# Scoring the last four heads of each attention batch as three fp32r products of split operands

## The chip, the cores and the metric

One core of one Trainium2 chip runs the whole program. The metric is the device time of one launch in microseconds; times given as a median come from several launches. Its engines are TensorE (PE, with its weight loads as PEld), VectorE (DVE), ScalarE (ACT), GpSimd (POOL) and SyncE (SP), which issues most of the DMAs.

## The reference

A batch of 64 sequences of 32 rows and 512 columns goes through three small linear maps whose weights are picked by an index of each sequence, and then through an attention layer with a paged cache. Attention is the part that matters here:

```python
q = rope(rmsnorm(x @ Wq)); k = rope(rmsnorm(x @ Wk)); v = x @ Wv
kc = k_cache[block_table].reshape(bsz, 512, 8, 128)
vc = v_cache[block_table].reshape(bsz, 512, 8, 128)
k_all = concatenate([kc, k], axis=1)
v_all = concatenate([vc, v], axis=1)
scores = einsum('bqhd,bkhd->bhqk', q, k_all) * SCALE
scores = where(valid, scores, -1e30)
probs = softmax(scores, axis=-1)
o = einsum('bhqk,bkhd->bqhd', probs, v_all)
return o.reshape(bsz, 32, 32 * 128) @ Wo.T
```

There are 32 query heads over 8 key heads, so four query heads of 32 rows share a key head and form 128 rows. Each sees 512 cached keys and 32 new ones, 544 in all. Everything is float32.

## The kernel before

The program runs its stages one after the other: preparation, maps, values, projection, attention, output. The change lies in `stage_attention`.

That stage walks over the 64 sequences, which are called batches here, two to a loop iteration (a pair). A pair has 16 steps `n`, one per key head; `j` is the batch within the pair and `h` the head, 0 to 7. Buffers that are kept twice are numbered by `j`. Each engine has its own written-out order of work and waits on semaphores for the others; nothing is reordered.

- **SP** loads, per batch, 16 key pages of 128 KB each and the new keys (L1056, L1057), the queries (L1058), then the new values of the batch before (L1065), and stores a finished batch (L1071). Key and query buffers are reused two batches on, so the load waits until the last head of the batch that used them is scored.
- **POOL** loads the cached values of the next batch with four indirect DMAs in heads 3 to 6 (L1106, L1110). In every head it multiplies the exponentials by the reciprocal of their sum (L1124), and every fourth head it does so for the 32 new keys of four heads together (L1129).
- **TensorE** in step n makes the scores of head n (L1147), turns the weights of head n-2 (L1157, every fourth head also the group of new ones, L1164), and weighs the values of head n-3 (L1179, every fourth head also the new values, L1188). The scores are two float32 products of 288 and 256 key columns, each of which becomes two matmul instructions on the chip.
- **DVE** takes the scores out of PSUM with the mask and the row minimum (L1273), copies the turned weights of head n-2 out of PSUM (L1283), and makes the reciprocal of head n's sum (L1287). In head 7 it also makes the mask of the next batch (L1256 to L1259).
- **ACT** makes the exponentials and their sum (L1214), copies the turned new weights (L1225) and the finished outputs (L1235) every fourth head.

The scores and the turned weights have two PSUM buffers each, and the exponentials a ring of eight. The output stage and the projection already multiply in this way: float32 operands are kept as a rounded high part and a low part, both of type fp32r, and three fp32r products are summed in PSUM (L1430, L824). ACT makes a high part by a copy (L1466), DVE a low part by a subtraction (L1487, L887).

## Time and profile before

| | us |
|---|---|
| median of 3 runs | 2527.35 (2525.82 to 2528.05) |
| the profiled execution, whole | 2534.27 |
| its span, first to last instruction | 2532.5 |
| TensorE busy in the span | 2423.1 |
| DVE, ACT, POOL busy | 1545.5, 1161.6, 1124.4 |
| attention stage, scores of the first to the last batch | about 851 to 2141 |
| mean granted TensorE clock, share of full | 0.983 |

The rows of a trace name the engine, the line of the kernel, the operation, and output and inputs by the program's names. Busy time of an engine is the sum of its instructions without overlap; matmuls are pipelined, so the distance between two starts says more of their price than the duration of one. Where an engine waits for a semaphore, the trace names the instruction that released it.

### The profile page before, as it was taken

What the parts mean: (1) busy time and instruction counts of PE and PEld (TensorE: products, weight loads), DVE (VectorE), ACT (ScalarE), POOL (GpSimd) and SP (SyncE); (2) the same over time, 40 slices, a digit from 0 to 9 for tenths busy, and PEclk for the clock granted to TensorE, in tenths of its full rate; (3) what the DMA queues carried; (4) which work ended last, traced back from release to release, by engine and by line L of the source; (5) the groups of instructions that cost most, each with busy time, mean ns of one, the idle gap of its engine ahead of it and who ended that gap; (6) DMA issues with size and microseconds to landing.
All of it is one profiled execution on the core that took longest, in us unless ns stands there. A gap on an engine that the chain in (4) does not pass through costs nothing. (4 is left out here: it accounts for less than half of the span.)

```text
span 2532.5 us, 52304 instructions
## 1 busy us (share of the span) xinstructions
PE 2423.1 (96%) x14785; PEld 2023.1 (80%) x14785; DVE 1545.5 (61%) x3027; ACT 1161.6 (46%) x2251; POOL 1124.4 (44%) x1364
## 2 busy tenths in 40 slices
PE   5989999999999599999999999999999999899999
PEld 4337777777776498999998999999989998788887
DVE  4656299888888466666666666666666665332221
ACT  6663387778777233433433344344333433321111
POOL 0323144444444466666666666666656665000000
PEclk9999999999999799999999999999999999999999
DMA  9334233333332788888888888888888885843442
GB/s 307 100 102 170 82 104 104 93 100 98 95 94 86 229 275 270 273 274 275 271 272 269 276 274 275 274 273 276 278 254 274 275 272 179 241 126 107 133 126 65
DMA packets 475258, 501.44 MB, mean 198 GB/s; under 512 B 104373, under 2 KB 399285, under 8 KB 471094
## 3 DMA queue, kind: packets, MB, share of 16 engines
q1 hardware_dynamic: 438326, 366.38, 47.2%
q0 software_dynamic: 36864, 134.23, 16.1%
q8 instruction: 32, 0.52, 0.1%
q14 instruction: 36, 0.29, 0.0%
HBM read 404.02 MB, written 96.47 MB: 198 GB/s over the span
## 5 line engine op out<-in xcount | busy, mean ns | idle before, releaser
L1214 ACT ACTIVATE att_probs<-att_probs,att_low 128x544 f32<-128x544 f32 x512 | 383.2, 748 | 800.9 <-DVE att_low L1273 798.6
L1124 POOL TENSOR_TENSOR att_probs<-att_probs,att_inverse 128x512 f32<-128x512 f32 x512 | 534.4, 1044 | 392.1 <-DVE att_inverse L1287 388.7
L1273 DVE CUSTOM_DVE_ANT_0 att_probs<-att_score,att_mask,att_batch_cols 128x544 f32<-128x544 f32 x512 | 401.5, 784 | 340.7 <-PE att_score L1147 336.7
L1147 PE MATMUL att_score<-att_keys_raw,att_queries_raw 128*128 128x288 f32 (+1 forms) x2048 | 556.5, 395 | 29.9 <-DMA att_queries_raw<-q_t 29.9
L1179 PE MATMUL att_o<-att_probs_t,att_values 128*128 128x128 f32 x4096 | 541.0, 275 | 0.0
L1179 PEld LDWEIGHTS att_o<-att_probs_t,att_values 128*128 128x128 f32 x4096 | 497.6, 192 | 0.1
L1147 PEld LDWEIGHTS att_score<-att_keys_raw,att_queries_raw 128*128 128x128 f32 x2048 | 351.8, 192 | 85.4 <-DMA att_queries_raw<-q_t 31.0
L1283 DVE COPY att_probs_t<-att_turn 128x512 f32<-128x512 f32 x512 | 351.2, 686 | 1.3 <-PE att_turn L1157 1.3
L1157 PE MATMUL att_turn<-ident,att_probs 128*128 128x128 f32 x2048 | 307.8, 273 | 1.6 <-POOL att_probs L1124 1.5
L1157 PEld LDWEIGHTS att_turn<-ident,att_probs 128*128 128x128 f32 x2048 | 256.1, 141 | 54.5 <-POOL att_probs L1124 3.4
L1110 POOL DMA_INDIRECT att_values<-L_cond_v_cache,att_v_rows_of x256 | 251.5, 982 | 81.6 <-POOL att_v_rows_of L1106 49.7
L824 PE MATMUL proj_proj<-x3t_hi,proj_w_hi 128*128 128x512 f32 x640 | 266.5, 416 | 0.0
L824 PE MATMUL proj_proj<-x3t_hi,proj_w_lo 128*128 128x512 f32 x640 | 250.8, 392 | 0.0
L824 PE MATMUL proj_proj<-x3t_lo,proj_w_hi 128*128 128x512 f32 x640 | 250.1, 391 | 0.0
L970 POOL TENSOR_TENSOR proj_q_out<-proj_by_cos,proj_by_sin 128x512 f32<-128x512 f32 x128 | 165.3, 1292 | 172.6 <-DVE proj_by_sin L902 172.6
L1430 PE MATMUL out_y<-out_wot_hi,out_o_hi 128*128 128x512 f32 x512 | 200.2, 391 | 0.0
L1430 PE MATMUL out_y<-out_wot_lo,out_o_hi 128*128 128x512 f32 x512 | 199.4, 390 | 0.0
L1430 PE MATMUL out_y<-out_wot_hi,out_o_lo 128*128 128x512 f32 x512 | 199.4, 389 | 0.0
L1487 DVE TENSOR_TENSOR out_o_lo<-out_o_raw,out_o_hi 128x2048 fp32r<-128x2048 f32 x32 | 73.3, 2291 | 181.7 <-ACT out_o_hi L1466 181.7
L1287 DVE RECIPROCAL att_inverse<-att_total 128x1 f32<-128x1 f32 x512 | 83.4, 163 | 138.5 <-ACT att_probs L1214 138.5
L1466 ACT ACTIVATE out_o_hi<-out_o_raw 128x2048 fp32r<-128x2048 f32 x32 | 61.4, 1919 | 214.5 <-PE out_y L1430 181.3
L900 DVE TENSOR_TENSOR proj_by_cos<-proj_raw,rope 128x512 f32<-128x512 f32 x160 | 136.8, 855 | 37.5 <-ACT proj_raw L856 37.5
(130 smaller groups left out, 3204.7 us busy)
## 6 DMA issues: line engine op xcount, KB each, us to landing
att_keys_raw<-L_cond_k_cache SPq DMA_DIRECT2D x1024, 128.0 KB
q_t<-proj_q_out SPq DMA_DIRECT2D x32, 1024.0 KB, 3.9
att_queries_raw<-q_t SPq DMA_DIRECT2D x64, 512.0 KB
o_t<-att_heads_out SPq DMA_DIRECT2D x64, 512.0 KB, 5.3
out_o_raw<-o_t SPq DMA_DIRECT2D x32, 1024.0 KB, 5.8
prep_natural<-L_cond_weight SPq DMA_DIRECT2D x16, 1024.0 KB, 8.6
w_nat<-L_cond_Wq SPq DMA_DIRECT2D x8, 1024.0 KB, 5.9
v_new<-values_v_out SPq DMA_DIRECT2D x16, 512.0 KB, 2.6
```

What stands on the lines that cost most here:

```text
L824: last = nc.tensor.matmul(proj_ps[t % RING][:], w[u][:, m, c, :], x[:, c, rc * 512:(rc + 1) * 512], start=(c == 0 and k == 0), stop=(c == ...
L900: nc.vector.tensor_tensor(by_cos[n][:], raw[n][:], rope[:, cos, cols], ALU.mult)
L970: nc.gpsimd.tensor_tensor(out, by_cos[n].rearrange("d (b s) -> d b s", s=S), by_sin[n].rearrange("d (b s) -> d b s", s=S), ALU.add).then_i ...
L1110: nc.gpsimd.indirect_dma_start(values[v][:, t, :], None, v_rows, bass.IndirectOffsetOnAxis(ap=v_rows_of[v][:, t:t + 1], axis=0)).then_inc( ...
L1124: nc.gpsimd.tensor_tensor(probs[:, k, 0:L], probs[:, k, 0:L], inverse[:, k:k + 1].to_broadcast([P, L]), ALU.mult).then_inc(probs_ready, 1)
L1147: last = nc.tensor.matmul(score_ps[n % 2][:, cols], queries_raw[j][:, h, :], keys_raw[j][:, pages, h, :], start=True, stop=True)
L1157: last = nc.tensor.transpose(turn_ps[job % 2][:, t * P:(t + 1) * P], probs[:, m % RING, t * P:(t + 1) * P], ident[:])
L1179: last = nc.tensor.matmul(o[:, cols], values[j][:, t, h * D:(h + 1) * D], probs_t[m % 2][:, t * P:(t + 1) * P], start=(h % GH == 0 and t = ...
L1214: nc.scalar.activation(probs[:, k, :], probs[:, k, :], ACT.Exp, bias=low[k][:, 0:1], scale=-1.0, accum_out=total[k][:, 0:1]).then_inc(exp_ ...
L1273: nc.vector.tensor_tensor_reduce(out=probs[:, k, :], in0=score_ps[n % 2][:, LEFT:LEFT + KEYS], in1=mask[j][:], scale=batch_cols[j][:, h:h ...
L1283: nc.vector.tensor_copy(probs_t[m % 2][:], turn_ps[job % 2][:]).then_inc(kept[job % 2], 1)
L1430: last = nc.tensor.matmul(y_ps[g][:], o[h % 2][:, r, rows].rearrange("d b s -> d (b s)"), w[:, hq, :], start=(hq == 0 and k == 0), stop=(h ...
```

## The change

Heads 4 to 7 of a batch (from `NATIVE` on) are no longer scored from the float32 keys and queries. Each operand is kept as a high and a low part of type fp32r, and per product of 288 or 256 columns three matmuls are summed: high by high, query high by key low, query low by key high. The parts of a batch are made in six pieces: five of pages (3, 3, 3, 4 and 4 pages of the four heads, so 384 or 512 columns) and one of queries (512 columns). ACT copies the high parts, pieces 0 to 3 in heads 4 to 7 of the batch before and pieces 4 and 5 in heads 0 and 1 of the batch itself. DVE subtracts for the low parts one head later each, pieces 0 to 2 in heads 5 to 7 and 3 to 5 in heads 0 to 2. TensorE waits before head 4 for all low parts. The mask of the next batch moves from head 7 to head 4 on DVE. SP's key load waits for head 4 of the batch that used the buffer, not head 7. For the first batch ACT makes pieces 0 to 3 and DVE 0 to 2 ahead of the loop; the last pair is written out, since it splits no next batch.

```diff
@@ -982,6 +982,11 @@
     GH = 4
     RING = 8
     PAIRS = B // 2
+    NATIVE = 4
+    ACT_FROM, DVE_FROM = 4, 5
+    SPLIT = HK - NATIVE
+    PARTS = [slice(0, 3), slice(3, 6), slice(6, 9), slice(9, 13), slice(13, NPP + 1)]
+    NP = len(PARTS)
     FIRST = NPP // 2 + 1
     LEFT = 512 - FIRST * PSIZE
     KLD = 16 * (NPP + 2)
@@ -993,6 +998,10 @@
         pages_sb = a_.sb("pages", [1, B * NPP], I32)
         keys_raw = [a_.sb(f"keys_raw{v}", [P, NPP + 1, HK, PSIZE]) for v in range(2)]
         queries_raw = [a_.sb(f"queries_raw{v}", [P, HK, P]) for v in range(2)]
+        keys_hi = [a_.sb(f"keys_hi{v}", [P, NPP + 1, SPLIT, PSIZE], F32R) for v in range(2)]
+        keys_lo = [a_.sb(f"keys_lo{v}", [P, NPP + 1, SPLIT, PSIZE], F32R) for v in range(2)]
+        queries_hi = [a_.sb(f"queries_hi{v}", [P, SPLIT, P], F32R) for v in range(2)]
+        queries_lo = [a_.sb(f"queries_lo{v}", [P, SPLIT, P], F32R) for v in range(2)]
         values = [a_.sb(f"values{v}", [P, PPT, KVD]) for v in range(2)]
         new_values = [a_.sb(f"new_values{v}", [P, HK, D]) for v in range(2)]
         v_rows_of = [a_.sb(f"v_rows_of{v}", [P, PPT], I32) for v in range(2)]
@@ -1014,6 +1023,8 @@
         pages_loaded = a_.sem("pages_loaded")
         keys_loaded = a_.sem("keys_loaded", 2)
+        hi_ready = a_.sem("hi_ready")
+        lo_ready = a_.sem("lo_ready")
         v_loaded = a_.sem("v_loaded", 2)
         new_loaded = a_.sem("new_loaded", 2)
         zeroed = a_.sem("zeroed")
@@ -1051,7 +1062,7 @@
                 if not first:
                     sp.wait_ge(pages_loaded, 16)
-                    sp.wait_ge(scores_done[1], (i - 1) * (N // 2) + (v + 1) * (HK // 2))
+                    sp.wait_ge(scores_done[NATIVE % 2], (i - 1) * (N // 2) + v * (HK // 2) + (NATIVE // 2 + 1))
                 for n in range(NPP):
                     sp.dma_start(keys_raw[v][:, n], kt[bass.ds(pages[n], 1)].rearrange("n d h k -> d (n h) k")).then_inc(keys_loaded[v], 16)
                 sp.dma_start(keys_raw[v][:, NPP], kn_dram[bass.ds(b, 1)].rearrange("b d h s -> d (b h) s")).then_inc(keys_loaded[v], 16)
@@ -1142,10 +1153,18 @@
                 j, h = divmod(n, HK)
                 if h == 0:
                     pe.wait_ge(keys_loaded[j], i * KLD + KLD)
+                if h == NATIVE:
+                    pe.wait_ge(lo_ready, i * (2 * NP + 2) + (j + 1) * (NP + 1))
                 pe.wait_ge(scores_masked[n % 2], i * (N // 2) + n // 2)
                 for pages, cols in ((slice(0, FIRST), slice(LEFT, 512)), (slice(FIRST, NPP + 1), slice(512, LEFT + KEYS))):
-                    last = nc.tensor.matmul(score_ps[n % 2][:, cols], queries_raw[j][:, h, :], keys_raw[j][:, pages, h, :],
-                                            start=True, stop=True)
+                    if h < NATIVE:
+                        last = nc.tensor.matmul(score_ps[n % 2][:, cols], queries_raw[j][:, h, :], keys_raw[j][:, pages, h, :],
+                                                start=True, stop=True)
+                        continue
+                    s = h - NATIVE
+                    for k, (q, kt_) in enumerate(((queries_hi, keys_hi), (queries_hi, keys_lo), (queries_lo, keys_hi))):
+                        last = nc.tensor.matmul(score_ps[n % 2][:, cols], q[j][:, s, :], kt_[j][:, pages, s, :],
+                                                start=(k == 0), stop=(k == 2))
                 last.then_inc(scores_done[n % 2], 1)
             def turn(i, n):
@@ -1208,6 +1227,15 @@
         @block.scalar
         def _(act):
+            def split(b, i, c, v):
+                if c == 0:
+                    act.wait_ge(keys_loaded[v], i * KLD + KLD)
+                if c < NP:
+                    nc.scalar.activation(keys_hi[v][:, PARTS[c]], keys_raw[v][:, PARTS[c], NATIVE:HK], ACT.Copy).then_inc(hi_ready, 1)
+                else:
+                    nc.scalar.activation(queries_hi[v][:], queries_raw[v][:, NATIVE:HK], ACT.Copy).then_inc(hi_ready, 1)
             def softmax(i, n):
                 act.wait_ge(scores_masked[n % 2], i * (N // 2) + (n // 2 + 1))
                 k = n % RING
@@ -1235,22 +1263,43 @@
                 nc.scalar.activation(heads_out[j][:, (g % 2) * GH:(g % 2 + 1) * GH].rearrange("d h n -> d (h n)"), o_ps[g % 2][:],
                                      ACT.Copy).then_inc(o_ready[g % 2], 1)
-            def pair(i, first):
+            def pair(i, first, last_pair):
                 for n in range(N):
+                    j, h = divmod(n, HK)
                     softmax(i, n)
+                    if HK - ACT_FROM + h <= NP:
+                        split(i * 2 + j, i, HK - ACT_FROM + h, j)
+                    if h >= ACT_FROM and not (last_pair and j == 1):
+                        if h == ACT_FROM:
+                            act.wait_ge(scores_done[1], i * (N // 2) + j * (HK // 2))
+                        split(i * 2 + (j + 1), i + j, h - ACT_FROM, (j + 1) % 2)
                     if n % GH == 1 and (n >= GH or not first):
                         new_part(i, n - 2)
                     if n % GH == 3 and (n >= GH or not first):
                         keep_o(i, n - 4)
-            pair(0, True)
-            with act.Fori(1, PAIRS) as i:
-                pair(i, False)
+            act.wait_ge(zeroed, 2)
+            for c in range(HK - ACT_FROM):
+                split(0, 0, c, 0)
+            pair(0, True, False)
+            with act.Fori(1, PAIRS - 1) as i:
+                pair(i, False, False)
+            pair(PAIRS - 1, False, True)
             new_part(PAIRS, -1)
             keep_o(PAIRS, -1)
         @block.vector
         def _(dve):
+            def split(b, c, v):
+                dve.wait_ge(hi_ready, b * (NP + 1) + (c + 1))
+                if c < NP:
+                    nc.vector.tensor_tensor(keys_lo[v][:, PARTS[c]], keys_raw[v][:, PARTS[c], NATIVE:HK], f32(keys_hi[v][:, PARTS[c]]),
+                                            ALU.subtract).then_inc(lo_ready, 1)
+                else:
+                    nc.vector.tensor_tensor(queries_lo[v][:], queries_raw[v][:, NATIVE:HK], f32(queries_hi[v][:]),
+                                            ALU.subtract).then_inc(lo_ready, 1)
             def columns(b, v):
                 cols = stat[:, bass.ds(b, 1), :].rearrange("p b c -> p (b c)")
                 nc.vector.reciprocal(batch_cols[v][:, 0:HK], cols[:, 0:HK])
@@ -1292,8 +1341,12 @@
                     mask_scores(i, n, first)
                     if n >= 2 or not first:
                         main_part(i, n - 2)
+                    if HK - DVE_FROM + h <= NP:
+                        split(i * 2 + j, HK - DVE_FROM + h, j)
                     if not (last_pair and j == 1):
-                        if h == HK - 1:
+                        if h >= DVE_FROM:
+                            split(i * 2 + (j + 1), h - DVE_FROM, (j + 1) % 2)
+                        elif h == DVE_FROM - 1:
                             dve.wait_ge(scores_masked[1], i * (N // 2) + j * (HK // 2))
                             columns(i * 2 + (j + 1), (j + 1) % 2)
                     invert(i, n)
@@ -1304,6 +1357,8 @@
                 nc.vector.memset(mask[v][:, L:KEYS], 0.0).then_inc(setup, 1)
             dve.wait_ge(setup, 3)
             columns(0, 0)
+            for c in range(HK - DVE_FROM):
+                split(0, c, 0)
             pair(0, True, False)
             with dve.Fori(1, PAIRS - 1) as i:
                 pair(i, False, False)
```

TensorE, heads 2 to 4 of a batch in the first pair. `att_turn` is the turn, `att_o` the weighing. Before:

```order
L1188 MATMUL att_o<-att_new_probs_t,att_new_values 128x128 x4
L1147 MATMUL att_score<-att_keys_raw,att_queries_raw 128x288
L1147 MATMUL att_score<-att_keys_raw,att_queries_raw 128x256
L1157 MATMUL att_turn<-ident,att_probs 128x128 x4
L1179 MATMUL att_o<-att_probs_t,att_values 128x128 x4
L1147 MATMUL att_score<-att_keys_raw,att_queries_raw 128x288
L1147 MATMUL att_score<-att_keys_raw,att_queries_raw 128x256
L1157 MATMUL att_turn<-ident,att_probs 128x128 x4
```

The same place now:

```order
L1207 MATMUL att_o<-att_new_probs_t,att_new_values 128x128 x4
L1161 MATMUL att_score<-att_keys_raw,att_queries_raw 128x288
L1161 MATMUL att_score<-att_keys_raw,att_queries_raw 128x256
L1176 MATMUL att_turn<-ident,att_probs 128x128 x4
L1198 MATMUL att_o<-att_probs_t,att_values 128x128 x4
L1166 MATMUL att_score<-att_keys_hi,att_queries_hi 128x288
L1166 MATMUL att_score<-att_keys_lo,att_queries_hi 128x288
L1166 MATMUL att_score<-att_keys_hi,att_queries_lo 128x288
L1166 MATMUL att_score<-att_keys_hi,att_queries_hi 128x256
L1166 MATMUL att_score<-att_keys_lo,att_queries_hi 128x256
L1166 MATMUL att_score<-att_keys_hi,att_queries_lo 128x256
L1176 MATMUL att_turn<-ident,att_probs 128x128 x4
```

Head 3 is scored as before; head 4 has six matmuls where two products stood, and turn and weighing keep their places.

DVE, heads 4 and 5 of the second batch of the first pair, as it is now (ISA stands for the masking and its minimum):

```order
L1322 ISA att_probs,att_low<-att_score,att_mask,att_batch_cols 128x544 [waits att_scores_done0,att_setup,att_turned1]
L1322 ISA att_low 128x1
L1332 COPY att_probs_t<-att_turn 128x512 [waits att_weighed0,att_turned0]
L1305 RECIPROCAL att_batch_cols<-stat 128x8 [waits att_scores_masked1]
L1306 COPY att_batch_cols<-stat 128x1
L1308 TENSOR_SCALAR att_mask<-att_key_no,att_batch_cols 128x512 [waits att_cols_ready]
L1336 RECIPROCAL att_inverse<-att_total 128x1 [waits att_exp_done]
L1322 ISA att_probs,att_low<-att_score,att_mask,att_batch_cols 128x544 [waits att_scores_done1,att_setup]
L1322 ISA att_low 128x1
L1332 COPY att_probs_t<-att_turn 128x512 [waits att_weighed1,att_turned1]
L1297 TENSOR_TENSOR att_keys_lo<-att_keys_raw,att_keys_hi 128x384 [waits att_hi_ready]
L1336 RECIPROCAL att_inverse<-att_total 128x1 [waits att_exp_done]
```

The subtraction stands between the copy out of PSUM and the reciprocal, and the three mask instructions stand in head 4 where before they stood in head 7.

ACT, heads 4 to 6 there, now:

```order
L1242 ACTIVATE att_probs,att_total<-att_probs,att_low 128x544 [waits att_scores_masked0]
L1235 ACTIVATE att_keys_hi<-att_keys_raw 128x384 [waits att_keys_loaded0,att_scores_done1]
L1242 ACTIVATE att_probs,att_total<-att_probs,att_low 128x544 [waits att_scores_masked1]
L1235 ACTIVATE att_keys_hi<-att_keys_raw 128x384
L1253 ACTIVATE att_new_probs_t<-att_turn 128x128 [waits att_o_done0,att_turned0]
L1242 ACTIVATE att_probs,att_total<-att_probs,att_low 128x544 [waits att_scores_masked0]
```

The first copy of the next batch's keys waits for their load, right behind the exponentials of head 4, and the exponentials of head 5 come behind it.

## Rows read from the trace of the kernel before

**Rows 1.** The page, busy time: share of the span and instructions of each engine.
```profile
PE 2423.1 (96%) x14785; PEld 2023.1 (80%) x14785; DVE 1545.5 (61%) x3027; ACT 1161.6 (46%) x2251; POOL 1124.4 (44%) x1364
```

**Rows 2.** Windows: stretch, its length, busy us of each engine, granted clock, DMA share, GB/s.
```profile
291.00:301.00 10.00, 7.70 (x27) 6.22 (x28) 3.46 (x5) 2.99 (x5) 0.20 (x1) 0.50 0.16 51
1400.00:1800.00 400.00, 400.00 (x2922) 367.08 (x2921) 259.80 (x700) 160.48 (x400) 262.51 (x300) 1.00 0.88 275
1878.00:1882.00 4.00, 4.00 (x19) 3.43 (x19) 0.86 (x3) 0.03 (x1) 0.00 (x0) 0.57 0.28 113
```

**Rows 3.** Timeline of TensorE near the attention's end: start us, us, engine, line, operation.
```profile
2089.26 1.06 PE L1188 MATMUL att_o<-att_new_probs_t,att_new_values 128*128 128x128 f32 x8
...
2102.40 1.08 PE L1147 MATMUL att_score<-att_keys_raw,att_queries_raw 128*128 128x288 f32 x4
2103.32 0.60 PE L1157 MATMUL att_turn<-ident,att_probs 128*128 128x128 f32 x4
2103.76 1.06 PE L1179 MATMUL att_o<-att_probs_t,att_values 128*128 128x128 f32 x8
2104.65 1.08 PE L1147 MATMUL att_score<-att_keys_raw,att_queries_raw 128*128 128x288 f32 x4
...
2109.26 1.06 PE L1188 MATMUL att_o<-att_new_probs_t,att_new_values 128*128 128x128 f32 x8
```

**Rows 4.** Timeline of TensorE, output stage: first and last of ten fp32r matmuls.
```profile
2299.83 0.39 PE L1430 MATMUL out_y<-out_wot_hi,out_o_lo 128*128 128x512 f32 x1
...
2301.87 0.39 PE L1430 MATMUL out_y<-out_wot_hi,out_o_lo 128*128 128x512 f32 x1
```

**Rows 5.** Timeline of one head in mid stage; in brackets idle time before and its releaser.
```profile
1512.75 1.05 POOL L1124 TENSOR_TENSOR att_probs<-att_probs,att_inverse 128x512 f32<-128x512 f32 x1
1512.90 0.78 DVE L1273 CUSTOM_DVE_ANT_0 att_probs<-att_score,att_mask,att_batch_cols 128x544 f32<-128x544 f32 x1 [0.49 <-PE att_score L1147]
...
1513.61 0.69 DVE L1283 COPY att_probs_t<-att_turn 128x512 f32<-128x512 f32 x1
1513.73 0.75 ACT L1214 ACTIVATE att_probs<-att_probs,att_low 128x544 f32<-128x544 f32 x1 [1.36 <-DVE att_low L1273]
...
1514.60 0.16 DVE L1287 RECIPROCAL att_inverse<-att_total 128x1 f32<-128x1 f32 x1 [0.31 <-ACT att_probs L1214]
...
1514.95 1.05 POOL L1124 TENSOR_TENSOR att_probs<-att_probs,att_inverse 128x512 f32<-128x512 f32 x1
```

**Rows 6.** Waits of TensorE in the whole run: total us, times, longest us.
```profile
PE att_score L1147 <- DMA att_queries_raw<-q_t: 29.9, 2, 29.1
...
PE att_o L1188 <- DMA att_new_values<-v_new: 7.9, 5, 2.7
...
PE proj_w L794 <- PEq L471: 4.4, 1, 4.4
...
PE att_turn L1157 <- POOL att_probs L1124: 1.5, 3, 0.8
```

**Rows 7.** Groups by form, whole run: busy us, mean ns of one.
```profile
L970 POOL TENSOR_TENSOR proj_q_out<-proj_by_cos,proj_by_sin 128x512 f32<-128x512 f32 x128 | 165.3, 1292 | 172.6 <-DVE proj_by_sin L902 172.6
L900 DVE TENSOR_TENSOR proj_by_cos<-proj_raw,rope 128x512 f32<-128x512 f32 x160 | 136.8, 855 | 37.5 <-ACT proj_raw L856 37.5
...
L1430 PEld LDWEIGHTS out_y<-out_wot_hi,out_o_hi 128*128 128x128 f32 x512 | 96.4, 188 | 19.8
...
L1487 DVE TENSOR_TENSOR out_o_lo<-out_o_raw,out_o_hi 128x2048 fp32r<-128x2048 f32 x32 | 73.3, 2291 | 181.7 <-ACT out_o_hi L1466 181.7
...
L887 DVE TENSOR_TENSOR proj_w_lo<-proj_w,proj_w_hi 128x512 fp32r<-128x512 f32 x40 | 27.5, 688 | 46.4 <-ACT proj_w_hi L844 46.3
```

**Rows 8.** Timeline at the end of the first batch.
```profile
861.46 0.75 ACT L1214 ACTIVATE att_probs<-att_probs,att_low 128x544 f32<-128x544 f32 x1 [1.17 <-DVE att_low L1273]
...
868.57 0.60 PE L1157 MATMUL att_turn<-ident,att_probs 128*128 128x128 f32 x4
...
870.89 1.18 PE L1147 MATMUL att_score<-att_keys_raw,att_queries_raw 128*128 128x288 f32 x4 [0.82 <-DMA att_queries_raw<-q_t]
```

## The prediction

> **What bounds the kernel now.** I read four views in this order: the busy shares, the windows, the timeline of TensorE, then the waits. TensorE is busy 96% of the span, the other engines 44 to 61% [rows 1]. In the middle of the attention stage it is busy all the time, at full granted clock, with DVE at 65%, ACT at 40%, POOL at 66% and the DMA engines at 88% [rows 2]. The timeline shows what fills it [rows 3]. The four matmul instructions that the two score products of a head become take 0.92 us (2102.40 to 2103.32), the turn 0.44 and the weighing 0.89, so a head takes 2.25. Four heads with their group turn and new-value products take 10.00, a batch of eight 20.00 (2089.26 to 2109.26). So each microsecond taken from the scores counts until another engine's work per batch, or a chain of waits, gets as long.
>
> The chain of one head [rows 5]: mask at 1512.90, exponent at 1513.73, reciprocal at 1514.60, POOL's product from 1514.95 to 1516.00, 3.1 us from the end of the scores to weights that can be turned. TensorE turns head n-2 after the scores of head n, two heads (4.5 us) later, so 1.4 us are spare. TensorE waited for POOL 1.5 us in the whole run [rows 6].
>
> **1. Scores of heads 4 to 7.** A native head's 0.92 us is four times its 544 columns at 2.4 GHz (2176 columns, 0.907) and a little. A split head makes six fp32r matmuls; by the 512-wide rows below each goes through once: 3 x 288 and 3 x 256 columns, 1632, 0.680 us at 2.4 GHz. What stands on top of each is not shown at this width. The only fp32r rows are 512 wide: nine intervals in 2.04 us (2299.83 to 2301.87), 0.2267 each, where 512 columns are 0.2133: 13.3 ns more [rows 4]. If that is a fixed price per matmul, a split head costs 0.680 + 6 x 0.0133 = 0.76, and saves 0.16. If it is a share (1/16), 0.72, saving 0.20. As the native rows have it (13 ns over four), 0.70, saving 0.22. Against it: keys are now read in runs of 32 columns at one column per tick, which no row shows; I bound that by half the overhead again, 0.80, saving 0.12. I take 0.16, by the nearest row of the same type. Of 256 split heads, the four of the first batch lie under a DMA wait (3). 252 x 0.16 = **-40.3 us** (ends -30 and -55).
>
> The Trainium skill (TensorE: Matmul & The Clock Gate, "Wait — 56ns, not 53.3ns?") gives N / 2.4 + 2.5 ns between warm matmuls. By it a split head would be an estimated 0.695 us, and this term -57. It also gives 215.8 ns for 512 columns, where this trace has 226.7, so I hold to the row.
>
> **2. New values come earlier.** TensorE waited five times, 7.9 us, for the new values [rows 6]. SP issues them behind the next batch's keys. These now go out once the fifth head's scores are done, not the eighth's, 6.7 us earlier, and the longest wait was 2.7. I take **-7.9 us** (ends 0 and -7.9).
>
> **3. The first batches.** ACT now reads the next batch's keys right behind the exponent of the fifth head. In the first batch that exponent starts at 861.46, but the second batch's keys only land at 870.8: TensorE waited for them until 870.89 [rows 8]. The exponent of head 5 is queued behind that wait and one copy (about 0.5): 871.3. Then 0.85 exponent with its accumulator, 0.2 reciprocal, 1.05 POOL, with hand-overs 873.5. TensorE turns head 5 then, not at 868.57 [rows 8]. Weighing (0.89) and turn (0.44) bring the second batch's first score to 874.9 instead of 870.89: **+4.0**. TensorE idles over 5 us there. After a wait of 4.4 us the clock was at its lower level, 1.2 GHz, in 291 to 301; after one of 2.7 us it was so for part of 1878 to 1882 [rows 2, 6]. I add **+3.0** for work at half clock (ends 0 and 5). Before the first head, four copies and three subtractions (about 2 us) lie beside its first scores, which run at half clock. I expect no such wait for the third batch's keys, whose request moves up by three heads.
>
> **4. What is hidden.** DVE: 259.8 us in 20 batches [rows 2] is 13.0 per batch. A subtraction of 512 columns is 0.69 and one of 2048 is 2.29 [rows 7], so 384 columns are 0.69 - 128 x 0.00104 = 0.56. Three of each add 3.7, sum 16.7, and the batch becomes 20.0 - 4 x 0.16 = 19.36. In one head: the copy out of PSUM ends at 1514.30, and the reciprocal waits for ACT until 1514.60 [rows 5]; a subtraction between them fills the 0.3 and delays the reciprocal by 0.3 to 0.4. The chain is then 3.5 us, two split heads are 4.2: cost nothing, 0.7 left. Without that cover each delay counts directly. The mask columns move from head 7 to 4, where no subtraction lies.
> ACT: six copies, each below the 0.75 exponent of 544 columns [rows 5], under 4.5 beside 8.0 busy per batch: nothing.
> POOL: a head with a value load takes 2.20 (1512.75 to 1514.95) [rows 5], more than a split head's 2.09. But TensorE's three heads there also hold a group turn and new-value products, 7.3 against 6.6. Nothing.
> The wait for the low parts, before head 4's first score: the last subtraction is made in head 2, some 2 us before. Nothing is queued behind it but TensorE's own work.
> DMA: the same bytes, 88% x 20.0 / 19.36 = 91%. The keys' window is the same: before, eighth head's scores to first score two batches on, 20.0 + 1.3 = 21.3; now from the fifth head's scores to ACT's fifth head one batch on, 19.4 + 1.8 = 21.2. Before, no key load was waited for past the second batch [rows 6]. But the value loads, issued in heads 3 to 6, now lie beside the keys' whole first half.
>
> **The sum:** -40.3 - 7.9 + 4.0 + 3.0 = -41.2 us. The profiled execution took 2534.27, so 2493.1; it stands 6.9 above the median of three, 2527.35. From the median: **2486 us**.
>
> **Rivals.**
> *A, slower: VectorE becomes the bound.* The subtraction of two SBUF operands may stand off against POOL's product. In the projection stage DVE's product of two SBUF operands takes 855 ns beside POOL's 1292, where a 512-column subtraction with a PSUM operand takes 688 [rows 7]: 0.17 more each, 1.0 per batch, 17.7, still under 19.36. It decides from (19.36 - 16.7) / 6 = 0.44 us per subtraction. If each waited a whole POOL product, 1.05, the batch would be 16.7 + 6.3 = 23.0, +3.0 x 64 = +192: 2719. Against it: POOL's product of the head before starts right behind the reciprocal and takes 1.05, while mask and copy ahead of the subtraction take 1.4.
> The Trainium skill (SBUF — State Buffer, "Who interferes with whom") says that a DVE instruction with two SBUF inputs and a GpSimd one that reads SBUF exclude each other for the whole instruction; by that rule this rival, if they meet.
> *B, slower: weight loads show.* An fp32r load takes 188 ns [rows 7], a matmul now 107 to 120. Unhidden, a head would be 6 x 0.188 = 1.13, +0.21 x 252 = +53: 2579. Against it: eight loads with matmuls as short take 0.89 [rows 3], 0.111 each.
> *C, faster: no fixed price.* Saving 0.22: -55.4 - 7.9 + 7 = -56: 2471.
> *D, no change: the keys come late.* If landing grows to 21.9 us, ACT waits in every batch and the period stays at 20.0: about 2527.
> *E: the split is not single-pass at this width.* Then a split head costs more than a native one; it ends as B, and is counted there.
>
> **Chances.** Forecast 0.60, C 0.24, D 0.05, A 0.06, B with E 0.05. From no change a measurement here can tell about 0.2%, 5 us. Faster takes the forecast, C and part of D, 0.86; within 0.2% 0.03; slower 0.11. Range: below, the lowest unknowns -55 - 7.9 + 0 = -63, 2464; above, -30, no new-value gain and +9 at the start give -21, 2506, and 0.12 us of DVE delay per batch would be 8 more: 2514. That leaves out the full cases A, B and D.
>
> **What would show it.** Score groups of 0.76 us in heads 4 to 7, batches of 19.36 between new-value products; new-value waits gone; one TensorE wait of about 5 us near 868 to 874 behind ACT's first copy of the second batch's keys; DVE near 86% in the steady stage. TensorE waiting for POOL in every batch would make me wrong by A, score groups over 0.92 by B, and ACT waiting for keys past the second batch by D.

## The result and the profile after

The changed kernel takes 2537.71 us (median of 20 runs, 2527.34 to 2545.63), the kernel before 2529.23 on the same chips (20 runs, 2521.2 to 2533.49). The ratio is 1.0033, with a 95% interval of 1.0022 to 1.0044: slower by 0.33%. The forecast was 2486. The profiled execution took 2537.59, its span is 2535.8, the mean granted clock 0.979.

The page of the changed kernel, busy us and share of the span, answers to [rows 1]:

```profile
PE 2397.7 (95%) x15297; PEld 2046.1 (81%) x15297; DVE 1723.9 (68%) x3411; ACT 1341.4 (53%) x2635; POOL 1135.6 (45%) x1364
```

The windows (length, busy us of PE, PEld, DVE, ACT, POOL, then granted clock, DMA share and GB/s), the middle of attention as in [rows 2]:

```profile
1400.00:1800.00 400.00, 385.55 (x3027) 366.70 (x3025) 309.23 (x805) 212.09 (x509) 261.35 (x296) 1.00 0.86 271
```

TensorE is busy for 25 us less in the whole run, and in the middle stretch it now stands idle for 14.45 us of 400, where it had no gap before [rows 2]. Work was taken away, and waits grew in its place. The timeline shows that the score groups came out as forecast. Last matmuls of one head's weighing, then a split head:

```profile
1507.51 1.06 PE L1198 MATMUL att_o<-att_probs_t,att_values 128*128 128x128 f32 x8
1508.33 0.38 PE L1166 MATMUL att_score<-att_keys_hi,att_queries_hi 128*128 128x288 f32 x1
1508.54 0.30 PE L1166 MATMUL att_score<-att_keys_lo,att_queries_hi 128*128 128x288 f32 x1
1508.68 0.30 PE L1166 MATMUL att_score<-att_keys_hi,att_queries_lo 128*128 128x288 f32 x1
1508.82 0.28 PE L1166 MATMUL att_score<-att_keys_hi,att_queries_hi 128*128 128x256 f32 x1
1508.93 0.28 PE L1166 MATMUL att_score<-att_keys_lo,att_queries_hi 128*128 128x256 f32 x1
1509.05 0.28 PE L1166 MATMUL att_score<-att_keys_hi,att_queries_lo 128*128 128x256 f32 x1
1509.17 0.60 PE L1176 MATMUL att_turn<-ident,att_probs 128*128 128x128 f32 x4
1509.61 1.06 PE L1198 MATMUL att_o<-att_probs_t,att_values 128*128 128x128 f32 x8
1510.42 0.38 PE L1166 MATMUL att_score<-att_keys_hi,att_queries_hi 128*128 128x288 f32 x1
```

From the weighing at 1507.51 to the turn at 1509.17 are 1.66 us; less the 0.89 of a weighing [rows 3], the six matmuls take 0.77 (forecast 0.76, native 0.92). The first starts 0.07 early, 0.82 after the weighing, and its distance to the second is 0.21. The other distances are 0.14 for 288 columns and 0.11 to 0.12 for 256, the columns at 2.4 GHz plus some 13 ns each, the price that the 512-column rows had [rows 4].

So each batch needs less of TensorE, but on the whole batches do not come faster. From one batch's new-value products to the next, mean of batches 10 to 60, were 20.19 us before and are **20.29** after (up to 20.36, by the batch at which one starts to count). From the first batch's to the last's are 1272.5 us before and 1272.9 after. The mean hides two things. After, the second to the ninth batch do follow each other at 19.37 us, the forecast's batch, and between 880 and 1030 us neither TensorE nor ACT waits for keys; only then do the waits begin. Before, 49 of the 63 distances are 20.00 to 20.05, TensorE's own, and the other 14 go up to 22.91. The waits say who is late (us in total, times, longest; 1200 to 2000 us):

```profile
ACT att_keys_hi L1235 <- DMA att_queries_raw<-q_t: 71.5, 35, 5.2
...
PEld att_o L1207 <- ACT att_new_probs_t L1253: 27.4, 15, 3.4
...
PE att_o L1207 <- ACT att_new_probs_t L1253: 19.6, 9, 3.2
...
PE att_o L1207 <- DMA att_new_values<-v_new: 6.8, 11, 2.0
```

ACT waits for the next batch's keys and queries in 35 of some 40 batches there, and behind ACT's wait stand its copy of the turned new weights and TensorE. This is the sign that the prediction named for rival D. But the reason is not slow landing. The timeline of SP, one cycle before and one after, shows it (SPq is SP's sequencer, here DMA issues only):

```profile
1496.08 8.18 SPq L1056 DMA_DIRECT2D att_keys_raw<-L_cond_k_cache  x16
1504.45 0.33 SPq L1057 DMA_DIRECT2D att_keys_raw<-k_new_t  x1
1504.96 0.38 SPq L1058 DMA_DIRECT2D att_queries_raw<-q_t  x1
1505.60 2.88 SPq L1065 DMA_DIRECT2D att_new_values<-v_new  x4
1508.76 0.38 SPq L1071 DMA_DIRECT2D o_t<-att_heads_out  x1
1516.32 0.86 SPq L1056 DMA_DIRECT2D att_keys_raw<-L_cond_k_cache  x2
```

```profile
1415.82 8.19 SPq L1067 DMA_DIRECT2D att_keys_raw<-L_cond_k_cache  x16
1424.19 0.33 SPq L1068 DMA_DIRECT2D att_keys_raw<-k_new_t  x1
1424.71 0.38 SPq L1069 DMA_DIRECT2D att_queries_raw<-q_t  x1
1425.34 2.88 SPq L1076 DMA_DIRECT2D att_new_values<-v_new  x4
1428.50 0.38 SPq L1082 DMA_DIRECT2D o_t<-att_heads_out  x1
1435.96 0.34 SPq L1067 DMA_DIRECT2D att_keys_raw<-L_cond_k_cache  x1
```

From one batch's first key issue to the next batch's are 20.24 us in this cycle of before and 20.14 in this one of after, and in neither is there a wait. Sixteen key issues take 8.2, the new keys and queries 1.2, the new values 2.9 and the store 0.4. Then 7.1 to 7.2 us pass in which no DMA is issued: SP reads the next batch's 16 page numbers from SBUF and tests the bounds of each. These are the instructions of the page-number read, after and before (ns least, median, most; first and last start):

```profile
L1060 SPq FUSED_REGOPS  x1054: 60/147/183, 828.9 to 2105.3; - x176
L1060 SPq SEQ_ASSERT  x1024: 18/18/37, 829.1 to 2105.5; - x171
L1060 SPq TENSOR_LOAD <-att_pages x64: 977/2476/2947, 827.6 to 2098.7; - x64
```

```profile
L1049 SPq FUSED_REGOPS  x1054: 60/147/183, 831.1 to 2101.1; - x176
L1049 SPq SEQ_ASSERT  x1024: 18/18/37, 831.4 to 2101.3; - x171
L1049 SPq TENSOR_LOAD <-att_pages x64: 978/2084/2925, 829.9 to 2095.3; - x64
```

The last row of each counts the whole stage: 63 cycles take 2098.7 - 827.6 = 1271.1 us after and 2095.3 - 829.9 = 1265.4 before, 20.18 and 20.09 each. In the kernel after SP sets this rhythm, once the keys that it asked for ahead are used up. In the kernel before it is nearly tied with TensorE's 20.00 and shows only where TensorE waits for new values (5 times, 7.9 us [rows 6]), in some of the 14 longer batches. Its waits for scores, before and after:

```profile
SPq L1056 <- PE att_score L1147: 7.2, 11, 1.7
```

```profile
SPq L1065 <- PE att_score L1166: 1.6, 1, 1.6
```

**SP's own issuing and register work takes as long as the batch of TensorE that it feeds.** Before, it waited for scores 11 times, for 7.2 us; now it is asked three heads earlier, and never has to wait past the first batches. The keys still go out when SP gets to them. Their landing is no slower: from a batch's first key issue to its last landing are 14.5 us after and 14.2 before (mean of batches 10 to 60).

### The profile page after: what moved, and what is told of

The parts are those of the page before. It is cut to its first block and busy times, and to the rows that moved or that the text cites. A ratio compares the mean times of both kernels' runs of the same rounds, so it can differ in the third digit from the quotient of the medians.

```text
span 2535.8 us, 54567 instructions
## 1 busy us (share of the span) xinstructions
PE 2397.7 (95%) x15297; PEld 2046.1 (81%) x15297; DVE 1723.9 (68%) x3411; ACT 1341.4 (53%) x2635; POOL 1135.6 (45%) x1364
## 5 line engine op out<-in xcount | busy, mean ns | idle before, releaser
L1161 PE MATMUL att_score<-att_keys_raw,att_queries_raw 128*128 128x288 f32 (+1 forms) x1024 | 279.5, 396 | 29.2 <-DMA att_queries_raw<-q_t 29.2
L1121 POOL DMA_INDIRECT att_values<-L_cond_v_cache,att_v_rows_of x256 | 263.1, 1028 | 82.1 <-POOL att_v_rows_of L1117 49.7
L1176 PEld LDWEIGHTS att_turn<-ident,att_probs 128*128 128x128 f32 x2048 | 247.2, 141 | 28.8 <-POOL att_probs L1135 3.5
L1297 DVE TENSOR_TENSOR att_keys_lo<-att_keys_raw,att_keys_hi 128x384 fp32r<-128x384 f32 (+1 forms) x320 | 198.3, 620 | 68.0 <-ACT att_keys_hi L1235 67.4
L1235 ACT ACTIVATE att_keys_hi<-att_keys_raw 128x384 fp32r<-128x384 f32 (+1 forms) x320 | 176.8, 553 | 124.1 <-DMA att_queries_raw<-q_t 124.1
L1161 PEld LDWEIGHTS att_score<-att_keys_raw,att_queries_raw 128*128 128x128 f32 x1024 | 177.1, 193 | 57.8 <-DMA att_queries_raw<-q_t 30.1
L1207 PE MATMUL att_o<-att_new_probs_t,att_new_values 128*128 128x128 f32 x1024 | 142.3, 283 | 37.6 <-ACT att_new_probs_t L1253 27.3
```

The costliest lines, as they stand in the source:

```text
L1121: nc.gpsimd.indirect_dma_start(values[v][:, t, :], None, v_rows, bass.IndirectOffsetOnAxis(ap=v_rows_of[v][:, t:t + 1], axis=0)).then_inc( ...
L1161: last = nc.tensor.matmul(score_ps[n % 2][:, cols], queries_raw[j][:, h, :], keys_raw[j][:, pages, h, :], start=True, stop=True)
L1176: last = nc.tensor.transpose(turn_ps[job % 2][:, t * P:(t + 1) * P], probs[:, m % RING, t * P:(t + 1) * P], ident[:])
L1235: nc.scalar.activation(keys_hi[v][:, PARTS[c]], keys_raw[v][:, PARTS[c], NATIVE:HK], ACT.Copy).then_inc(hi_ready, 1)
L1297: nc.vector.tensor_tensor(keys_lo[v][:, PARTS[c]], keys_raw[v][:, PARTS[c], NATIVE:HK], f32(keys_hi[v][:, PARTS[c]]), ALU.subtract).then_i ...
```

## The experiments

The theory, *SP's cycle*: per batch SP needs 20.1 to 20.3 us, so nothing taken from TensorE shows. Rivals: A, DVE's subtractions or their port; the start-up, where the second batch begins 4 us later; slow landing of the keys, for want of DMA bandwidth. Every kernel ran in five rounds beside the kernel before, and a ratio is to the kernel before on the same chip. On other chips that kernel's median differs by up to 7.5 us, so runs of different chips are compared by their ratios; the kernel after has 1.0033. Period is the mean distance of new-value products, batches 10 to 60, good to about 0.05 where batches vary.

### Relieving SP: e1_after_nocheck and e2_before_nocheck

The bounds tests of the page numbers are left out, in the kernel after (e1) and in the one before (e2); nothing else changes. The page numbers are then trusted.

```diff
-  pages_sb[0:1, bass.ds(b * NPP, NPP)], engines=(mybir.EngineType.SP,), min_val=0, max_val=PAGES - 1)
+  pages_sb[0:1, bass.ds(b * NPP, NPP)], engines=(mybir.EngineType.SP,), min_val=0, max_val=PAGES - 1,
+  skip_runtime_bounds_check_because="page numbers are drawn below PAGES")
```

> The changed kernel with SyncE's bounds checks on the 16 page numbers of a batch left out (4.06 us of its register work per batch; same DMAs, same bytes). SyncE theory: its own issue cycle, 20.2 us per batch, set the end; without up to 4 us of it TensorE sets it again at 19.4 us per batch, so about 2537 - 60 x 0.85 = 2487 us. DMA-bandwidth theory: no change, 2535 to 2540. VectorE or port theory: no change, 2535 to 2540.

> The kernel before with the same bounds checks left out. SyncE theory: SyncE and TensorE were nearly tied there (20.2 and 20.0 us per batch), so about 60 x 0.2 = 12 us faster at most, 2517, with no waits for new values left. DMA-bandwidth theory: no change, 2529.

Measured: e1 **2481.4** us (2480.22 to 2482.55), ratio 0.9795 (0.9782 to 0.9809), period 19.38. e2 2518.07 us, ratio 0.9941 (0.9928 to 0.9955), period 20.00. The windows of e1, then of e2:

```profile
1400.00:1800.00 400.00, 400.00 (x3188) 383.31 (x3187) 324.65 (x847) 223.55 (x537) 279.34 (x312) 1.00 0.86 283
```

```profile
1400.00:1800.00 400.00, 400.00 (x2922) 367.12 (x2921) 259.92 (x701) 160.47 (x401) 262.99 (x301) 1.00 0.87 275
```

SP's waits for scores, e1 then e2:

```profile
SPq L1068 <- PE att_score L1167: 140.2, 59, 3.9
```

```profile
SPq L1057 <- PE att_score L1148: 238.6, 60, 5.3
```

In e1 TensorE has no gap, SP waits in nearly every batch, and the period is 19.38, where the prediction worked out 19.36. The same DMAs now move 283 GB/s, where the kernel after had 271, and from a batch's first key issue to its last landing are 16.8 us, longer than the 14.5 after, while ACT waits for keys only once, at the start. So neither bandwidth nor slow landing held the kernel after. With SP relieved on both sides the change is worth 2518.07 - 2481.4 = 36.7 us, against 40.3 in its first term. So the edit on TensorE did what was forecast, and SP hid it. The kernel before had lost 0.59% to SP already (14 us against the 2532.37 of the kernel before on that chip); of this the new-value waits, 7.9 us [rows 6], were what TensorE showed.

### Loading SP: e3_before_more and e5_after_more

```diff
+  nc.values_load_multi_w_load_instructions(
+      pages_sb[0:1, bass.ds(b * NPP, 4)], engines=(mybir.EngineType.SP,), min_val=0, max_val=PAGES - 1)
```

> The kernel before with one more read of four page numbers into registers per batch on SyncE (about 1.0 + 4 x 0.25 = 2.0 us of its time, no DMA). SyncE theory: it was already the longest cycle, so nearly all of it shows: 62 x 2.0 = +124 us, 2650. TensorE theory (SyncE has slack): no change, 2529.

> The changed kernel with the same extra read of four page numbers per batch on SyncE as in the run on the kernel before (which took 2632). SyncE theory: both kernels are then set by the same cycle of SyncE alone, so this one takes about the same, 2632 to 2650. TensorE theory: it would keep its distance to a shorter TensorE cycle, under 2600.

Measured: e3 2631.93, ratio 1.0395 (1.0381 to 1.0409), period 21.62; e5 2638.29, ratio 1.0418 (1.0399 to 1.0436), period 21.73. The second read is worth some 1.5 us per batch, less than I had supposed for it, but it counts in full and alike: 3.95% over the kernel before (99.6 us) and 1.0418 / 1.0033, 3.84%, over the one after. Two kernels that differ by 0.6 us of TensorE work per batch take the same time, as near as the overlapping intervals tell, as soon as SP's work is the same and longest. In e3 TensorE waits for the new values, which SP issues behind the keys and queries:

```profile
PE att_o L1190 <- DMA att_new_values<-v_new: 64.6, 31, 5.0
```

### VectorE: e4_after_nolow and e9_nocheck_nolow

Both leave out the six subtractions; the low parts are zeros, so the scores of heads 4 to 7 lack them. e4 keeps SP's tests, e9 doesn't.

```diff
-  dve.wait_ge(hi_ready, b * (NP + 1) + (c + 1))
...
+  pass
...
+  nc.vector.memset(f32(keys_lo[v][:]), 0.0)
```

> The changed kernel without VectorE's six subtractions per batch: the low parts are zeroed once and multiplied as they stand, so the scores of heads 4 to 7 lose their low parts; TensorE waits for the high parts instead. VectorE or port theory: 3.7 us of VectorE per batch gone, about 2490. SyncE or DMA theory: no change, 2532 to 2540.

> The changed kernel without the bounds checks and without VectorE's subtractions (the low parts are zeroed once, some 5 us of VectorE at the start, and the scores of heads 4 to 7 lose them). If the subtractions are hidden, the period stays 19.38 us per batch and the time 2481 to 2487. If they cost TensorE something through the chain or through GpSimd, the period falls to 19.3 or less and the time by 5 us or more.

Measured: e4 2552.64, ratio 1.0076 (1.0062 to 1.009), period 20.46; e9 2480.87, ratio 0.9793 (0.9779 to 0.9806), period 19.37. Taking 56 of DVE's 325 us in the window (next row) away gains nothing with SP's tests, and without them nothing that can be told from noise (0.9793 against e1's 0.9795). Rival A falls at four split heads, and the subtractions are hidden as forecast:

```profile
1400.00:1800.00 400.00, 400.00 (x3188) 383.39 (x3187) 268.66 (x726) 223.84 (x538) 272.40 (x311) 1.00 0.87 284
```

That e4 is slower than the kernel after by 0.43%, some 11 us, was expected by no theory. 5 lie at the start, where DVE zeroes the low parts (first new-value products at 874.4, not 869.4); the period says where the rest is (below, with e10).

### The start: e8_late_first and e10_late_first_checks

In the first batch alone, ACT's and DVE's first pieces for the second batch come behind head 7 instead of beside heads 4 to 7; e8 without SP's tests, e10 with them.

```diff
-  if h >= ACT_FROM and not (last_pair and j == 1):
+  if h >= ACT_FROM and not (last_pair and j == 1) and not (first and j == 0):
...
+  if first and n == HK - 1:
+      act.wait_ge(scores_done[1], 0 + (HK // 2))
+      for c in range(HK - ACT_FROM):
+          split(1, 0, c, 1)
...
```

> The changed kernel without the bounds checks, and with the second batch's first pieces (ScalarE's 0 to 3, VectorE's 0 to 2) made after head 7 of the first batch, not in heads 4 to 7. This tests the start-up term: TensorE no longer stands for 4 to 5 us behind ScalarE's wait for the second batch's keys. Expected if that term was right: 3 to 6 us under the 2481 of the same kernel without this edit, 2475 to 2478, the rest taken by the pieces made in a row. If the start-up costs nothing: 2481.

> The changed kernel with all bounds checks kept, and the second batch's first pieces made after head 7 of the first batch. It asks where the 8 us come from by which the changed kernel is slower than the one before. Start-up theory: TensorE's wait of 4 us in the first batch goes straight to the end, so this kernel takes 2531 to 2534. SyncE theory: SyncE's cycle runs on through that wait and sets the end, so no change: 2535 to 2540.

Measured: e8 2481.71, ratio 0.9803 (0.979 to 0.9817), the same as e1. The expected gain of 3 to 6 us had a false premise: e1 has no such stall, its second batch begins at 868.18. e10 2553.4, ratio 1.0069 (1.005 to 1.0088), period 20.40 to 20.54; the start-up theory had said 2531 to 2534, SP's 2535 to 2540. Neither came: e10 is 0.36% slower than the kernel after. So the start does not explain the 8 us: where the first pieces come late nothing is gained, and in e10 SP's cycle is again longer. The kernel after shows the same without an experiment: its stall puts it 2.6 us behind the kernel before at the first new-value products (869.4 against 866.8), and at the ninth batch's it is 3.1 us ahead (1026.7 against 1029.8).

The parts of SP's cycle, mean us of batches 10 to 60, summed from the starts and durations of its instructions (waits for scores stand in "tests+wait", the read is the instruction that fetches the 16 page numbers; in e3 and e5 "tests+wait" holds the second read too):

```
                     keys  new k+q  new v  store  read  tests+wait  cycle
before               8.45    1.17   3.21    .72   2.10    4.55      20.19
after                8.42    1.17   3.22    .72   2.38    4.40      20.31
e1 (no tests)        8.97    1.18   4.09    .71   1.83    2.63      19.41
e2 (no tests)        8.57    1.17   3.18    .71   2.11    4.26      20.00
e3 (before, more)    8.44    1.21   3.20    .70   2.26    5.88      21.69
e5 (after, more)     8.50    1.25   3.15    .71   2.23    5.88      21.73
e4 (no subtract.)    8.40    1.20   3.23    .68   2.38    4.59      20.48
e10 (late first)     8.39    1.20   3.22    .70   2.33    4.64      20.48
```

Before, 0.14 of the 4.55 is waiting, so SP's own work there is 20.05 per batch, and 20.31 after. In e1 some 2.4 of the 2.63 are waiting (140.2 us in 59 waits). So the tests take some 4.1 us per batch, and 0.3 more of the 4.4 are other register work. What differs between the kernels that keep their tests is small change in SP's reading: the read of the page numbers 2.10 against 2.33 to 2.38, and up to 0.25 in the tests.

### Moving SP's work: e6_after_actnv

SP keeps its tests, but the four new-value loads of a batch are issued by ACT in head 3, behind its exponential.

```diff
-  load_new_values(0, i * 2, i * 2 - 1, False)
...
+  if h == 3 and not (first and j == 0) and not (last_pair and j == 1):
+      new_values_of(i * 2 + (j + 1), (j + 1) % 2)
```

> The changed kernel with all bounds checks kept, but the four loads of new values of a batch issued by ScalarE instead of SyncE (3.2 us of SyncE's cycle gone, some 3 us more on ScalarE, which is at 53%; same bytes, same number of DMAs). SyncE theory, whatever the time is spent on: 20.3 - 3.2 = 17.1 us is under TensorE's 19.4, so as without the checks, about 2481, and a little more if ScalarE is late in the head where it issues. Theory that the bounds checks alone, or the number of DMAs, are the matter: no change, 2538.

Measured: 2515.95 (2514.59 to 2517.11), ratio 0.9926 (0.9913 to 0.994), period 19.81. SP is relieved, and waits for scores 55 times (91.6 us). But e6 is only 1.1% faster than the kernel after, where e1 is 2.4% faster. Timeline of ACT and its queue (ACTq):

```profile
1439.87 0.75 ACT L1243 ACTIVATE att_probs<-att_probs,att_low 128x544 f32<-128x544 f32 x1 [2.30 <-DVE att_low L1325]
1440.04 0.57 ACTq L1237 DMA_DIRECT2D att_new_values<-v_new  x1
...
1440.62 0.58 ACT L1264 ACTIVATE att_heads_out<-att_o 128x512 f32<-128x512 f32 x1
1440.77 2.03 ACTq L1237 DMA_DIRECT2D att_new_values<-v_new  x3
1442.91 0.75 ACT L1243 ACTIVATE att_probs<-att_probs,att_low 128x544 f32<-128x544 f32 x1 [1.72 <-DVE att_low L1325]
```

The issues take 0.57 us each (median; up to 0.73), and the exponential queued behind the four starts 1.72 us after ACT fell idle; in the mean of batches 10 to 60 it is 1.79 us, and the exponential starts 0.11 us behind the last issue. The prediction's 1.4 us of slack in a head's chain [rows 5] cannot hold that: between 900 and 2080 us TensorE's weight loads waited for POOL's product 60 times, once a batch, 25.7 us in all, which is the 0.43 per batch that e6's period stands above e1's. I had priced the issues as hidden.

### More split heads: e7_after_n2_nocheck and e11_n3_nocheck

Six (e7) and five (e11) heads split instead of four, without SP's tests; the cut is e7's, e11 has 3 and 3, 4.

```diff
-  NATIVE = 4
-  ACT_FROM, DVE_FROM = 4, 5
+  NATIVE = 2
+  ACT_FROM, DVE_FROM = 2, 3
```

> The changed kernel without the bounds checks and with six heads split instead of two fewer (heads 2 to 7, high parts made in heads 2 to 7 and low parts in heads 3 to 7 and 0). TensorE theory: 2 x 0.155 us per batch less, 19.07 us per batch, -20 us against the 2481 of four split heads: 2461. VectorE theory: its six pieces take half as much again, 13.0 + 5.2 = 18.2 us per batch, and in a head 0.75 stands against 2.09, so TensorE starts to wait for it: 2475 to 2500.

> The changed kernel without the bounds checks and with five heads split (3 to 7; pieces of 480 and 640 columns). TensorE theory: one more split head is 0.155 us per batch less, -10 us against four: 2471. VectorE theory: the subtractions of two SBUF operands grow and run into GpSimd's products, as with six split heads (2492), where VectorE was busy 94%: with five about 90%, so half of the gain at best or none, 2475 to 2485.

Measured: e7 2492.03, ratio 0.9834 (0.9819 to 0.9849), period 19.50; e11 2480.93, ratio 0.9781 (0.9766 to 0.9795), period 19.36. The window of e7, then groups by form of e7 (count, busy us, mean ns) and of e11:

```profile
1400.00:1800.00 400.00, 399.19 (x3251) 382.25 (x3250) 375.51 (x844) 244.97 (x535) 294.02 (x309) 1.00 0.87 281
```

```profile
L1122 POOL DMA_INDIRECT att_values<-L_cond_v_cache,att_v_rows_of x256 | 328.0, 1281 | 82.2 <-POOL att_v_rows_of L1118 49.7 <-issue 32.3
...
L1298 DVE TENSOR_TENSOR att_keys_lo<-att_keys_raw,att_keys_hi 128x576 fp32r<-128x576 f32 x192 | 185.4, 966 | 19.1 <-ACT att_keys_hi L1236 19.1
L1298 DVE TENSOR_TENSOR att_keys_lo<-att_keys_raw,att_keys_hi 128x768 fp32r<-128x768 f32 x128 | 181.2, 1417 | 0.0
```

```profile
L1298 DVE TENSOR_TENSOR att_keys_lo<-att_keys_raw,att_keys_hi 128x480 fp32r<-128x480 f32 x192 | 196.3, 1023 | 18.7 <-ACT att_keys_hi L1236 18.7
...
L1298 DVE TENSOR_TENSOR att_keys_lo<-att_keys_raw,att_keys_hi 128x640 fp32r<-128x640 f32 x128 | 108.3, 846 | 0.0
```

With six heads DVE is busy 94% and is the likeliest bound, as in rival A: TensorE's own work would allow 19.38 - 2 x 0.15 = 19.08. Its weight loads waited for POOL's products 92 times, 23.0 us in all, between 900 and 2080 us, where in e1 they did so twice. That is 0.38 a batch, most of the 0.42 between 19.50 and 19.08. At the prediction's price (0.56 at 384 columns, 1.04 ns for each more) 576 columns would be 0.76 us and 768 columns 0.96; they take 0.97 and 1.42. In e11 480 columns take longer than 640: what counts is where the subtraction lies. In e7, 126 of the 192 subtractions of 576 columns overlap a POOL product and take 1.08 us in the mean; the 66 that overlap none take 0.75, nearly the prediction's price. A fifth split head therefore gains nothing that can be measured (0.9781 against 0.9795 in e1, intervals overlapping), though TensorE has 0.15 us less to do. That DVE holds it back there, at 89% busy, is argued, not shown. The four-head kernel with SP relieved, e1, is as fast as any measured, with one split head less than e11.

## Why the prediction was wrong

**The step that failed** is the last sentence of its first paragraph, with the list of its fourth part: each microsecond taken from the scores counts "until another engine's work per batch, or a chain of waits, gets as long", and the work per batch was then summed for DVE, ACT, POOL and DMA only. SP was not summed. Its issues and register work are not counted as busy, so no busy share shows them, and its own work was 20.05 us per batch before the change, level with TensorE's 20.00. The sum had no room for a gain beyond the first batches, which did come at 19.37; e1 and e2 show that, and e3 and e5 from the other side. This is the whole miss: the forecast was -41 us against the profiled run, the measured change 8.5 slower, and with SP relieved on both sides it is -36.7.

- *Scores, -40.3.* Right in mechanism and nearly in size: 0.77 instead of 0.76 per head, 36.7 us between e2 and e1. It just did not reach the end of the kernel. The fixed 13 ns per matmul was right for fp32r at these widths, so rival C falls. Here the Trainium skill (TensorE: Matmul & The Clock Gate, "Wait — 56ns, not 53.3ns?"), with N / 2.4 + 2.5 ns, does not fit fp32r: 122.5 and 109.2 ns, where the rows have 133 and 120.
- *New values, -7.9.* Wrong for the same reason. They lie behind the keys on SP, which gets there no earlier: 11 such waits, 6.8 us, from 1200 to 2000 us, where the kernel before had 4, 6.4 us. In e1 they are gone.
- *Start-up, +4.0 and +3.0.* The rows come close: the second batch's first score is at 874.71 (forecast 874.9), and the granted clock was 0.50, its lower level, from 867.4 to 874.2, after TensorE had stood idle since 865.2. But the path was another, so the near hit is luck in part. TensorE stood for 4.12 us behind ACT's copy of the turned new weights, not behind the turn of head 5, as the timeline has it:

```profile
867.38 0.52 ACT L1235 ACTIVATE att_keys_hi<-att_keys_raw 128x384 fp32r<-128x384 f32 x1 [7.21 <-DMA att_queries_raw<-q_t]
...
868.96 0.26 ACT L1253 ACTIVATE att_new_probs_t<-att_turn 128x128 f32<-128x128 f32 x1
...
869.36 2.05 PE L1207 MATMUL att_o<-att_new_probs_t,att_new_values 128*128 128x128 f32 x8 [4.12 <-ACT att_new_probs_t L1253]
...
874.71 1.08 PE L1161 MATMUL att_score<-att_keys_raw,att_queries_raw 128*128 128x288 f32 x4
```

  And it is no term of the sum while SP sets the rhythm: by the ninth batch it is made up. Nor is it one in e1, where it does not arise.
- *What is hidden.* DVE, ACT, POOL: right at four heads: DVE by experiment (e9 against e1, 2480.87 and 2481.4), ACT and POOL by e1, where TensorE has no gap. DVE's share came out at 81% in e1, not 86: six subtractions add 324.65 - 268.66 = 56 us in 400, 2.7 per batch and not 3.7, since a duration overlaps that of its neighbour. "The keys' window is the same" supposed that SP asks for the keys when the scores allow it. It asks when it is done with the batch before.
- *Rival D*, with 0.05, had the form: ACT waits for the keys in each batch, about 2527. Its condition, a slower landing, was not met (14.5 us against 14.2, and 16.8 in e1, where ACT does not wait); the same wait came from a late request.
- *Slower by 0.33%.* This is in part argued. SP's read of the page numbers took 0.28 us longer per batch in the kernel after, and the 0.14 of waiting went; the cycle is 0.12 longer (20.31 against 20.19). Over 63 cycles that would be some 7 of the 8.5 us between the medians, an estimate. Of the two profiled executions the kernel after's is only 3.3 us longer, and its SP takes 5.7 more over the stage (1271.1 against 1265.4) but starts 2.3 earlier. What lengthens the read **stays open**. e4 (2.38) shows that it is not the subtractions, e10 (2.33) that it is not the order of the start. e3, which has no split at all, reads in 2.26 and e5 in 2.23, so ACT's copies are not needed for a long read; and where SP waits for scores, it is often shorter (1.83 in e1), but not always (2.39 in e7). No run took ACT's copies away alone. The same holds for the 0.36% of e10 over the kernel after.

## What to carry to other kernels

Sum the time that every engine's instruction stream takes per iteration, the issuing engine's too, from the start of an instruction to the start of the same one an iteration later; if that distance has no wait in it, that engine is a bound, whatever its busy share. Look for it before the longest engine is shortened: two streams of 20.00 and 20.05 us look like one bottleneck, and a saving on the one that shows is worth nothing until the other is relieved. A few iterations may still come at the new rate, as the second to ninth batch did here, while work asked for ahead lasts; so measure the rhythm late in a loop. Here one argument of one call gave four times as much with the change (ratio 1.0033 to 0.9795) as without it (1 to 0.9941).

## What the runs showed of the hardware that was not expected

- SP's register work has a price: a read of 16 page numbers takes 1.83 to 2.39 us (means of the runs) and the tests of 16 numbers some 4.1, with a key issue every 0.52 us. In the kernel before, 2.1 for the read and 4.4 for tests and other register work are 6.5 of SP's 20.2 us. The Trainium skill (Perfetto Trace Analysis, "What "DMA-bound" means") has an issuing engine as the bound where its sequencer track is solid DMA slices. That sign is not there in this trace: the stretches of issues, with the gaps in them, cover 12.2 of 20.1 us in the cycle above, the issue instructions alone 8.9 (mean of batches 10 to 60), and SP was the bound all the same.
- DMA issues on ACT hold up the activations queued behind them: in e6 the next exponential starts 0.11 us after the fourth issue, with ACT idle for 1.79 before it (means).
- DVE's subtraction of two SBUF operands is stretched beside POOL's products: in e7 576 columns take 1080 ns where they overlap one and 748 where they don't. The other way, POOL's value loads were issued in 982 ns each before, 1062 in e1, 1281 in e7, and again 982 in e9, which is e1 without the subtractions. The Trainium skill (SBUF — State Buffer, "Who interferes with whom") has the two engines exclude each other where DVE has two inputs in SBUF and POOL reads SBUF. On the products the rows agree in kind. At four heads it cost no time that can be measured; at six, e7 is slower than e1.
